# An adaLN block on eight cores: the order of TensorE's work per attention head and per expert

## The reference

```python
h = _layernorm(x, axis=-1) * (1 + ca) + sa
x = x + ga * _L0_attn_ref(h, ...)      # attention over 3 blocks of 128 keys, projection, MLP of width 4096
h = _layernorm(x, axis=-1) * (1 + cb) + sb
x = x + gb * _L0_ffn_ref(h, ...)       # below

# in the attention: kk, vv are the previous, own and next block of 128 keys
sim = jnp.einsum('bnid,bnjd->bnij', q, kk)
sim = jnp.where(valid, sim, neg)
attn = jax.nn.softmax(sim, axis=-1)
out = jnp.einsum('bnij,bnjd->bnid', attn, vv)

# in the experts: x is h, N_EXPERTS = 8, D_EXPERT = 512
gates = _top_k_softmax(logits, TOP_K)
h = jax.nn.gelu(jnp.einsum('bsd,edh->bseh', x, w1) + b1, approximate=False)
expert_out = jnp.einsum('bseh,ehd->bsed', h, w2) + b2
out = jnp.einsum('bse,bsed->bsd', gates, expert_out)
```

## Time and profile before

| | |
|---|---|
| median of three runs | 3824.49 us (3818.71 to 3826.97) |
| the profiled execution | 3818.53 us |
| its span, slowest core (core 6) | 3817.0 us |
| spans of the eight cores | 3800.8 to 3817.0 us |
| PE busy over the span | 1866.2 us (49%) |
| DVE, ACT busy | 942.2 us (25%), 747.1 us (20%) |
| DMA engines, mean busy share | 0.20, 65 GB/s |
| granted PE clock, mean | 0.73 of full speed |
| idle of PE before L841 (V), put down to DVE L834 | 272.3 us in 256 waits |
| idle of PE before L1502 (T of the tail), put down to DVE L1495 | 233.1 us in 128 waits |
| idle of PE before L1516 (F2), put down to ACT L1507 | 111.7 us in 128 waits |

### The profile page before, as it was taken

How to read it: one execution, slowest core, us unless ns; L and a number is a source line. 1 busy time by engine, 2 the same in 40 slices (tenths; PEclk the granted TensorE clock), 3 DMA queues, 4 the chain that set the end, 5 groups by cost and what they waited for, 6 DMA issues and landing times.

```text
span 3817.0 us, 33532 instructions; the slowest of 8 cores (3800.8 to 3817.0 us)
## 1 busy us (share of the span) xinstructions
PE 1866.2 (49%) x10290; PEld 930.0 (24%) x10437; DVE 942.2 (25%) x2186; ACT 747.1 (20%) x1633; POOL 35.3 (1%) x68
## 2 busy tenths in 40 slices
PE   0405533654444444443478876700115666666665
PEld 0102211222222222212245554400112222222222
DVE  3252234213333333323321112122441011011011
ACT  0122222212111211111132222200221111111111
POOL 0000000000000000001100000000000000000000
PEclk9657766865555555556688888855558999999999
DMA  8231111131211111016510110155110000000000
GB/s 266 74 108 55 55 62 70 64 96 50 67 56 41 54 56 55 29 67 184 169 61 34 34 36 37 39 160 180 71 56 33 14 28 28 14 28 28 14 28 12
DMA packets 107772, 249.47 MB, mean 65 GB/s; under 512 B 29865, under 2 KB 44337, under 8 KB 105550
## 3 DMA queue, kind: packets, MB, share of 16 engines
q1 hardware_dynamic: 74544, 170.20, 14.4%
q10 hardware_dynamic: 27938, 60.33, 4.1%
q0 software_dynamic: 5120, 16.78, 1.3%
HBM read 186.95 MB, written 60.32 MB: 65 GB/s over the span
## 4 chain that ended last, share of the span: by engine, by line
PE 41%; DVE 19%; ACT 14%; DMA 12%; issue 11%; ACTq 1%; DVEq 1%; SPq 0%; PEldq 0%; PEld 0%; POOLq 0%
PE bank L1516 7%; PE bank L1482 5%; PE bank L1137 5%; PE bank L1116 5%; DMA arena<-w_in 4%; PE bank L651 4%; DMA arena<-wfc2T 3%; ACT arena L887 3%; DVE arena L834 2%; PE bank L873 2%; PE bank L914 2%; PE bank L841 2%; ACT arena L1507 2%; ACT arena L1491 2%; DMA arena<-wmod 2%
## 5 line engine op out<-in xcount | busy, mean ns | idle before, releaser
L1137 PE MATMUL bank<-arena 128*128 128x256 bf16 x2048 | 286.1, 287 | 175.8 <-DVE arena L1050 99.4
L1516 PE MATMUL bank<-arena 128*128 128x512 bf16 x992 | 261.8, 408 | 112.5 <-ACT arena L1507 111.7
L1137 PEld LDWEIGHTS bank<-arena 128*128 128x128 bf16 x2048 | 209.3, 103 | 264.7 <-issue 184.4
L1116 PE MATMUL bank<-arena 128*128 128x512 bf16 x968 | 260.6, 387 | 13.7 <-ACT arena L1145 11.0
L1495 DVE TENSOR_SCALAR arena<-arena 128x512 bf16<-128x512 f32 x128 | 62.2, 486 | 768.2 <-ACT arena L1491 768.2
L1482 PE MATMUL bank<-arena 128*128 128x512 bf16 x1002 | 240.3, 382 | 5.3 <-DMA arena<-s_h2T 3.5
L841 PE MATMUL bank<-arena 128*128 128x64 bf16 x768 | 81.5, 230 | 272.3 <-DVE arena L834 272.3
L887 ACT ACTIVATE arena<-bank 128x384 bf16<-128x384 f32 x256 | 125.4, 491 | 417.5 <-PE bank L873 333.5
L1145 ACT ACTIVATE arena<-bank,arena 128x256 bf16<-128x256 f32 x256 | 120.8, 475 | 411.1 <-PE bank L1137 411.0
L1491 ACT ACTIVATE arena<-bank 128x512 f32<-128x512 f32 x128 | 76.4, 597 | 591.8 <-PE bank L1485 501.3
L633 PE MATMUL bank<-ident_bf,arena 128*128 128x128 bf16 x144 | 18.2, 307 | 346.8 <-DVE arena L627 346.8
(11 more groups left out here) (161 smaller groups left out, 2081.6 us busy)
## 6 DMA issues: line engine op xcount, KB each, us to landing
arena<-wmod SPq DMA_DIRECT2D x16, 1536.0 KB, 8.7
arena<-x_ext SPq DMA_DIRECT2D x34, 512.0 KB, 5.2
arena<-wfc2T POOLq DMA_DIRECT2D x64, 256.0 KB, 4.2
arena<-wfc1T SPq DMA_DIRECT2D x64, 256.0 KB, 4.4
arena<-w_in SPq DMA_DIRECT2D x64, 256.0 KB, 2.7
arena<-w_in SPq DMA_DIRECT2D x32, 512.0 KB, 4.5
arena<-s_s SPq DMA_DIRECT2D x32, 512.0 KB, 5.0
arena<-wqkvT SPq DMA_DIRECT2D x16, 768.0 KB, 5.6
```

What stands on the lines that cost most here:

```text
L1116: st=tT_r[mu % 2]: e.matmul(bf(b)[:, :], st[:, l * 128:(l + 1) * 128], wfc2_bf[:, mm * 1024 + nn * 512: mm * 1024 + nn * 512 + 512], start ...
L1137: e.matmul(bf(b)[:, 0:256], wfc1_bf[:, kk * DFF + mm * 128: kk * DFF + mm * 128 + 128], zt[:, kk * 256:(kk + 1) * 256], start=(kk == 0), s ...
L1516: b=obks[n]: e.matmul(bf(b)[:, :], tT_bf[ii % 2][:, ts(kk, 128)], w2_bf[:, (ee * 4 + kk) * 1024 + nn * 512: (ee * 4 + kk) * 1024 + nn * 51 ...
```

## The change

It changes two loops and nothing else. The arithmetic, the instructions' sizes and their number stay as they are.

In the attention stage `emit_ptv` is split in two. `emit_tr_copy(h)` holds T and C, and `emit_v(h)` holds V and, after the heads 7 and 15, DVE's scaling. At head h the code now emits S(h), E(h), T(h-1), C(h-1), V(h-2). The transposes go to bank 2 and bank 5 by turns, and the buffers of the weights and of their transposes are three each in place of two. Two waits are left out: ACT's for the transposes of two heads before, and DVE's for V of two heads before.

In the expert tail T and C move into `tail_trc(e)` and F2 into `tail_fc2(e)`. At expert e the code now emits F1(e), the GELU and the gate's factor of e, T(e-1), C(e-1), F2(e-2). The transposed buffers are three in place of two. The wait for the weights is made once ahead of the loop, and that for the tile's input once in a tile.

```diff
@@ buffers of the attention stage @@
-    p_sb = [A.alloc(f"psb{i}", [128, WIN], BF16) for i in range(2)]
-    pT_sb = [A.alloc(f"pTsb{i}", [128, WIN], BF16) for i in range(2)]
+    p_sb = [A.alloc(f"psb{i}", [128, WIN], BF16) for i in range(3)]
+    pT_sb = [A.alloc(f"pTsb{i}", [128, WIN], BF16) for i in range(3)]
@@ attention, per head @@
-        def emit_ptv(idx):
+        def emit_tr_copy(idx):
+            tb = 2 if idx % 2 == 0 else 5
+            waitr("tensor", SEXP, idx + 1)
+            waitr("tensor", SPTE, idx - 1)
+            for j in range(3):
+                E.op("tensor", lambda e, jj=j, pp=p_sb[idx % 3], b=tb:
+                     e.transpose(
+                         bb(b)[:, jj * 128:(jj + 1) * 128],
+                         pp[:, jj * 128:(jj + 1) * 128], ident_bf[:, :]),
+                     inc=SPT.bump() if j == 2 else None)
+            E.wait("vector", SPT, SPT.n)
+            E.op("vector", lambda e, pt=pT_sb[idx % 3], b=tb: e.tensor_copy(
+                pt[:, :], bb(b)[:, 0:WIN]), inc=SPTE.bump())
+
+        def emit_v(idx):
             hh = idx % HEADS
             tt = idx // HEADS
             hf = hh // 8
             so = hh % 8
-            waitr("tensor", SEXP, idx + 1)
-            waitr("tensor", SPTE, idx)
-            for j in range(3):
...
-            E.wait("vector", SPT, SPT.n)
-            waitr("vector", SVM2, idx - 1)
...
-            E.wait("tensor", SPTE, SPTE.n)
+            waitr("tensor", SPTE, idx + 1)
             if so == 0:
                 waitr("tensor", SOEV, 8 * ((tt * 2 + hf) - 1))
...
             E.wait("scalar", SSC, SSC.n)
-            waitr("scalar", SPT, idx - 1)
...
             if h > 0:
-                emit_ptv(idx - 1)
-        emit_ptv(t * HEADS + HEADS - 1)
+                emit_tr_copy(idx - 1)
+            if h > 1:
+                emit_v(idx - 2)
+        emit_tr_copy(t * HEADS + HEADS - 1)
+        emit_v(t * HEADS + HEADS - 2)
+        emit_v(t * HEADS + HEADS - 1)
@@ expert tail @@
-    tT_bf = [A.alloc(f"tTbf{i}", [128, DEXP], BF16) for i in range(2)]
+    tT_bf = [A.alloc(f"tTbf{i}", [128, DEXP], BF16) for i in range(3)]
...
+    E.wait("tensor", WCE, wce_total)
...
+        def tail_trc(idx):
+            waitr("tensor", SSCL, idx + 1)
+            waitr("tensor", STTE, idx - 1)
+            for c in range(4):
+                E.op("tensor", lambda e, cc=c, ii=idx: e.transpose(
+                    bb(2 + ii % 2)[:, ts(cc, 128)],
+                    tEg_bf[ii % 2][:, ts(cc, 128)], ident_bf[:, :]),
+                    inc=STT.bump() if c == 3 else None)
+            E.wait("scalar", STT, STT.n)
+            E.op("scalar", lambda e, ii=idx: e.activation(
+                tT_bf[ii % 3][:, :], bb(2 + ii % 2)[:, 0:512], AF.Copy),
+                inc=STTE.bump())
+
+        def tail_fc2(idx):
+            ee = idx % NEXP
+            waitr("tensor", STTE, idx + 1)
+            if ee == 0:
+                waitr("tensor", SYEV, t - 1)
+            for n in range(2):
+                for k in range(4):
+                    E.op("tensor", lambda e, kk=k, nn=n, ee2=ee, ii=idx,
...
         for e_ in range(NEXP):
             idx = t * NEXP + e_
             bk = idx % 2
-            E.wait("tensor", WCE, wce_total)
-            wdma("tensor", ("h2b", t))
+            if e_ == 0:
+                wdma("tensor", ("h2b", t))
             waitr("tensor", SGEL, idx - 1)
...
-            E.wait("tensor", SSCL, SSCL.n)
-            waitr("tensor", STTE, idx - 1)
-            for c in range(4):
...
-            E.wait("tensor", STTE, STTE.n)
-            if e_ == 0:
-                waitr("tensor", SYEV, t - 1)
...
+            if e_ > 0:
+                tail_trc(idx - 1)
+            if e_ > 1:
+                tail_fc2(idx - 2)
+        tail_trc(t * NEXP + NEXP - 1)
+        tail_fc2(t * NEXP + NEXP - 2)
+        tail_fc2(t * NEXP + NEXP - 1)
```

More of the change, by code:

```diff
@@ L824, in emit_ptv @@
             so = hh % 8
-            waitr("tensor", SEXP, idx + 1)
-            waitr("tensor", SPTE, idx)
-            for j in range(3):
-                E.op("tensor", lambda e, jj=j, pp=p_sb[idx % 2]: e.transpose(
-                    bb(2)[:, jj * 128:(jj + 1) * 128],
-                    pp[:, jj * 128:(jj + 1) * 128], ident_bf[:, :]),
-                    inc=SPT.bump() if j == 2 else None)
-            E.wait("vector", SPT, SPT.n)
-            waitr("vector", SVM2, idx - 1)
-            E.op("vector", lambda e, pt=pT_sb[idx % 2]: e.tensor_copy(
-                pt[:, :], bb(2)[:, 0:WIN]), inc=SPTE.bump())
-            E.wait("tensor", SPTE, SPTE.n)
+            waitr("tensor", SPTE, idx + 1)
             if so == 0:
@@ L840, in emit_ptv @@
                 E.op("tensor", lambda e, jj=j, sl=(tt + j) % 4, h2=hh, hf2=hf,
-                     pt=pT_sb[idx % 2]: e.matmul(
+                     pt=pT_sb[idx % 3]: e.matmul(
                          bf(3 + hf2)[:, (h2 % 8) * 64:((h2 % 8) + 1) * 64],
@@ L884, in build_program @@
             E.wait("scalar", SSC, SSC.n)
-            waitr("scalar", SPT, idx - 1)
-            E.op("scalar", lambda e, b=scb, hh=h, pp=p_sb[idx % 2]:
+            E.op("scalar", lambda e, b=scb, hh=h, pp=p_sb[idx % 3]:
                  e.activation(pp[:, :], bf(b)[:, 0:WIN], AF.Exp,
@@ L1473, in build_program @@
         obks = (4, 5) if (t % 2 == 0) else (6, 7)
+        def tail_trc(idx):
[18 more added lines that the diff above has]
+                    E.op("tensor", lambda e, kk=k, nn=n, ee2=ee, ii=idx,
+                         b=obks[n]: e.matmul(
+                             bf(b)[:, :], tT_bf[ii % 3][:, ts(kk, 128)],
+                             w2_bf[:, (ee2 * 4 + kk) * 1024 + nn * 512:
+                                   (ee2 * 4 + kk) * 1024 + nn * 512 + 512],
+                             start=(ee2 == 0 and kk == 0), stop=False))
         for e_ in range(NEXP):
@@ L1498, in build_program @@
                 inc=SSCL.bump())
-            E.wait("tensor", SSCL, SSCL.n)
-            waitr("tensor", STTE, idx - 1)
-            for c in range(4):
-                E.op("tensor", lambda e, cc=c, ii=idx: e.transpose(
-                    bb(2 + ii % 2)[:, ts(cc, 128)],
-                    tEg_bf[ii % 2][:, ts(cc, 128)], ident_bf[:, :]),
-                    inc=STT.bump() if c == 3 else None)
-            E.wait("scalar", STT, STT.n)
-            E.op("scalar", lambda e, ii=idx: e.activation(
-                tT_bf[ii % 2][:, :], bb(2 + ii % 2)[:, 0:512], AF.Copy),
-                inc=STTE.bump())
-            E.wait("tensor", STTE, STTE.n)
-            if e_ == 0:
-                waitr("tensor", SYEV, t - 1)
-            for n in range(2):
-                for k in range(4):
-                    E.op("tensor", lambda e, kk=k, nn=n, ee=e_, ii=idx,
-                         b=obks[n]: e.matmul(
-                             bf(b)[:, :], tT_bf[ii % 2][:, ts(kk, 128)],
-                             w2_bf[:, (ee * 4 + kk) * 1024 + nn * 512:
-                                   (ee * 4 + kk) * 1024 + nn * 512 + 512],
-                             start=(ee == 0 and kk == 0), stop=False))
+            if e_ > 0:
[5 more added lines that the diff above has]
+        tail_fc2(t * NEXP + NEXP - 1)
         for n in range(2):
```

## The result

The changed kernel takes 3156.6 us (median of ten runs, 3150.4 to 3243.1) where the kernel before took 3825.7 in as many. The ratio is 0.826, with a 95% interval of 0.824 to 0.828. The forecast was 3150 us.

What follows compares the result with a forecast made beforehand. Attention and the expert tail were each taken as bound by a chain of waits going round between engines. 3818.5 - 384 (tail) - 290 (attention) = 3144.5, plus 6 us to the median, gave 3150 us, range 3105 to 3215.

Steps and rivals of the forecast that it cites:

- The tail: Expert tail: becomes a row of PE work, 34.1 us a tile, 546 to 548 us in all, gain 384 us.
- the cause given for it: Tail tile's end: the next GELU waits behind ACT's wait for the output, leaving PE 0.84 us idle before T.
- the rival of a throttled tail: Expert tail: a quarter of its 547 us at the lower clock, about 137 us more, 3290 us; chance 0.08.
- The Trainium skill's rule: Expert tail: die held at 13/16 of the clock under dense load, tail 123 us longer, total about 3273 us.
- Attention's ring: Attention heads: S(h), E(h), reciprocal(h), C(h-1), V(h-1), S(h+1) take 2.25 us; spanning two heads, 1.13 us a head.
- The prediction's own sum for a clock that stays low: Attention: 14 tiles gaining 16.4 us and 2 masked tiles gaining 17 us at the low clock, 264 us.
- the first rival: Attention: the heads stay at 1.2 GHz, gain 264 us in place of 290, total 3176 us; chance 0.34.
- the likeliest case: Whole kernel: granted clock in attention above 0.8, attention gains 290 us, total 3150 us; chance 0.50.
- the term of 290 us: Attention: gain taken between 264 us at the low clock and 344 us at the high end.
- Slower: Whole kernel: denser stages use up a clock budget, tail and MLP lose, up to 4184 us; chance 0.02.
- half the ring kept: Attention: C or V waits on something else, half the idle time stays, 130 us less gain, 3280 us; chance 0.05.

Runs made afterwards that it cites:

- the swap in the kernel before: In the kernel before, DVE does the copy C(h-1) ahead of the reciprocal of head h, PE's order unchanged: 3738.0 us, ratio 0.974.

## Why the prediction was right

**The tail.** It was forecast at 384 us and lost 383.8 on core 6. A tile was forecast at 34.1 us and takes 34.10; the wait before its first T was forecast at 0.84 us and is 10.5 / 15 = 0.70. The run with the output on SP shows that this wait has the cause given for it. The clock reached 1.00, against the rival of a throttled tail. The Trainium skill's rule in "TensorE: Matmul & The Clock Gate", the clock gate part, on a die whose third core starts dense matmuls, which the prediction weighed, did not show in this trace: 1.00 over the 555 us on core 3, and 1.00 on each of the eight cores from 2620 to 3110 us.

**Attention's ring.** The mechanism was as read, and the swap in the kernel before shows it directly. The number was off: 1.13 us a head was forecast and 1.065 came. The step that failed is "Third buffers and the second transpose bank only keep the waits for reuse off the ring", with the waits behind it costed at nothing. They cost 0.12 us in a ring of 2.25, 0.06 a head after the change.

**How 264 at the low clock became 285.** The prediction's own sum for a clock that stays low was 264 us. Core 6, from the first S to the MLP's first matmul:

| part | forecast, us | measured, us |
|---|---|---|
| first to last exponential of each tile | 264 | 264.3 |
| last exponential to last V | 0 | 14.2 |
| last V to the next tile's first exponential | 0 | 6.3 |
| behind the last tile | 0 | 0.5 |

The first line is right through errors that cancel. The forecast took 1.12 us off each of 15 intervals between exponentials. But the first interval is 0.48 us before and 0.47 after, because S of the heads 0 and 1 stand ahead of the first T in both orders, so 14 intervals had something to lose. They lost about 1.19 each, since the two waits are gone. The scaling costs 0.69 us now and cost 0.5, which is 0.2 more where 0.4 had been charged: 14 x 1.19 - 0.2 = 16.4 us a tile, the very number of 15 x 1.12 - 0.4.

The second line is a step that failed: "What stays the same is the tile's start [...] and the end (V(15) still waits on C(15), then scaling, transposes, projection)". V(15) does wait for C(15), but C(15) comes earlier, as T(15) no longer stands behind V(14). That is 0.89 us a tile. The third line is mostly the projection, whose matmuls ran longer at the higher clock in some tiles. From the last V of a tile to the next S it took 11.3 to 11.6 us before, and takes 10.1 to 11.8 after; no run was made on what sets that moment.

**The clock.** The forecast had it rise in the heads, and it did not: 0.50 in every stretch of 2 us of unmasked heads that was looked at, with PE busy throughout. Here the first rival was right, and the likeliest case wrong. The step that failed is "The new heads keep PE busy at 97%, which is nearer to the projection than to the old heads". PE busy without a gap did not raise the clock here; with S over 128 rows in place of 64 it rose, with PE busy for 1.67 of 2.00 us. So the term of 290 us came out near the measured 285 through errors that cancel: 26 us too much for a clock that stayed low, and 21 us too little for the ends of the tiles and the stretches between them. That part of the agreement is luck.

**Slower, and half the ring kept.** Neither came. The MLP's stage and the weights' loading were within 4 us of their old length on core 6.

## What to carry to other kernels

Trace the ring of waits instruction by instruction and look at the order inside each engine: the reciprocal ahead of the copy cost 0.39 us a head, and could have been had without any new pipeline depth. When a ring is stretched over two iterations, the next limit is often the sum of one engine's own work, here 3% away, so an experiment that adds work has to be read against that slack. After such a change look for the idle time at the edges of the tile: taking it away was worth 92 us here. And count how often the ring really repeats in a tile: here it was 14 times and not 15, and the end of the tile had a chain of its own.
